# Attention on one core: where GpSimd's copy of the shared tail stands, and what it is written into

## What is computed

```python
hidden_states = jnp.concatenate([context, latents], axis=1)
q = (latents @ Wq).reshape(b, q_len, N_KV_HEADS, N_GROUPS, HEAD_DIM)
k = (hidden_states @ Wk).reshape(b, kv_len, N_KV_HEADS, HEAD_DIM)
v = (hidden_states @ Wv).reshape(b, kv_len, N_KV_HEADS, HEAD_DIM)
scores = jnp.einsum('bqhgd,bkhd->bhgqk', q, k) * scale
attn = jax.nn.softmax(scores.astype(jnp.float32), axis=-1).astype(q.dtype)
out = jnp.einsum('bhgqk,bkhd->bqhgd', attn, v)
```

## Time and profile before

| | |
|---|---|
| median of 3 runs | 3725.41 us (3724.01 to 3728.13) |
| the profiled execution | 3725.45 us, its span 3723.7 us |
| TensorE busy over the span | 3479.5 us (93%) |
| VectorE, ScalarE, GpSimd busy | 2323.2, 1415.3, 837.3 us |
| attention stage | about 1195 to 2005 us from the span's start |
| granted clock of TensorE | 0.973 in the mean; 1.00 in the middle of the attention |

### The profile page before, as it was taken

How to read it: one execution, slowest core, us unless ns; L and a number is a source line. 1 busy time by engine, 2 the same in 40 slices (tenths; PEclk the granted TensorE clock), 3 DMA queues, 4 the chain that set the end, 5 groups by cost and what they waited for, 6 DMA issues and landing times. The chain is left out here.

```text
span 3723.7 us, 52261 instructions
## 1 busy us (share of the span) xinstructions
PE 3479.5 (93%) x18370; PEld 3066.9 (82%) x18370; DVE 2323.2 (62%) x3935; ACT 1415.3 (38%) x2648; POOL 837.3 (22%) x1100
## 2 busy tenths in 40 slices
PE   6999999899999999999998999999799999699899
PEld 5888888799998888888887787787689999677676
DVE  5555575877665777777775333332578888566765
ACT  4333343444333777777775222221411111221321
POOL 0000000000002667666662100000011111233231
PEclk8999999899999999999999999999899999899999
DMA  3333333454444333333334545543334443698986
GB/s 124 100 105 97 99 98 90 115 134 115 121 121 124 103 108 90 105 104 108 105 86 145 144 118 154 154 119 93 110 116 150 143 154 137 254 287 277 302 285 199
DMA packets 525094, 520.73 MB, mean 140 GB/s; under 512 B 177668, under 2 KB 413188, under 8 KB 524884
## 3 DMA queue, kind: packets, MB, share of 16 engines
q1 hardware_dynamic: 489220, 391.06, 35.5%
q0 software_dynamic: 34608, 124.90, 10.1%
q10 hardware_dynamic: 1056, 2.10, 0.2%
HBM read 402.95 MB, written 115.02 MB: 139 GB/s over the span
## 5 line engine op out<-in xcount | busy, mean ns | idle before, releaser
L2083 PE MATMUL wo_acc<-wo_w,wo_l 128*128 128x512 f32 (+1 forms) x2496 | 573.7, 392 | 21.9 <-DVE wo_l L2033 21.8
L427 PE MATMUL kv_bank<-kv_wo,kv_so 128*128 128x512 f32 x2436 | 575.7, 396 | 15.8 <-DVE kv_wo L519 10.6
L2083 PEld LDWEIGHTS wo_acc<-wo_w,wo_l 128*128 128x128 f32 (+1 forms) x2496 | 460.2, 185 | 135.2 <-DVE wo_w L2057 24.7
L427 PEld LDWEIGHTS kv_bank<-kv_wo,kv_so 128*128 128x128 f32 x2436 | 458.7, 190 | 110.6 <-issue 16.7
L815 PE MATMUL pr_bank<-pr_xo,pr_wp 128*128 128x400 f32 x2688 | 500.6, 348 | 27.5 <-ACT pr_s L882 11.9
L815 PEld LDWEIGHTS pr_bank<-pr_xo,pr_wp 128*128 128x128 f32 x2688 | 495.4, 191 | 30.4 <-DVE pr_wp L899 22.6
L2312 PE MATMUL w_acc<-w_w,w_l 128*128 128x512 f32 (+1 forms) x1848 | 451.5, 404 | 60.9 <-DVE w_l L2287 60.0
L2312 PEld LDWEIGHTS w_acc<-w_w,w_l 128*128 128x128 f32 (+1 forms) x1848 | 344.8, 189 | 167.3 <-DVE w_l L2287 36.9
L26 PE MATMUL hid_acc<-x1t,hid_w 128*128 128x336 f32 x2688 | 442.6, 323 | 1.4 <-DVE c_raw L1827 0.9
L26 PEld LDWEIGHTS hid_acc<-x1t,hid_w 128*128 128x128 f32 x2688 | 426.4, 194 | 2.1 <-issue 1.1
L1311 PE MATMUL outs<-pt,v 128*128 128x384 f32 (+3 forms) x1536 | 347.3, 348 | 27.9 <-issue 14.0
(11 more groups left out here) (185 smaller groups left out, 4182.3 us busy)
## 6 DMA issues: line engine op xcount, KB each, us to landing
wo_l_raw<-o_scratch SPq DMA_DIRECT2D x192, 256.0 KB, 2.9
w_l_raw<-h_scratch SPq DMA_DIRECT2D x140, 256.0 KB, 4.6
pair_raw<-in_L_xattn_Wq_dram SPq DMA_DIRECT2D x64, 512.0 KB, 5.6
q_scratch<-pr_out SPq DMA_DIRECT2D x128, 200.0 KB, 2.4
o_scratch<-o_stage SPq DMA_DIRECT2D x64, 400.0 KB, 3.5
q_raw<-q_scratch SPq DMA_DIRECT2D x64, 384.0 KB, 3.2
stage<-in_ctx_dram SPq DMA_DIRECT2D x45, 512.0 KB, 3.9
h_scratch<-c_raw SPq DMA_DIRECT2D x28, 672.0 KB, 5.5
```

The costliest lines, as they stand in the source:

```text
L427: last = pe.matmul(bank[:, BANK[i], :], so[:, i, a, c, :], wo[:, i, e, c, :], start=(not opened and c == 0 and (a, e) == PAIRS[0]), stop=( ...
L2083: last = pe.matmul(acc[p][:rows, :], l[j % 2][:, a, k, :rows], w[:, c, m * per + k, :], start=(m == 0 and k == 0 and (a, c) == PAIRS[0]), ...
```

## The change

`pt` is replaced by three tiles: `pt_first` (384 columns, one buffer) for the first half of a group and `pt_second0` and `pt_second1` (416 columns) for the second half, of which even and odd groups use one each. The copy of the tail into the second half waits for the product of the group before last, which used the same buffer. In GpSimd's loop it stands behind the scaling of tile I where tile I - 4 is the second of the group. Matmuls, copies and their sizes stay as they are.

```diff
-        pt = sb("pt", [P, 2, NC, cols], F32R)
+        pt_first = sb("pt_first", [P, 2, NC, split], F32R)
+        pt_second = [sb(f"pt_second{i}", [P, 2, NC, cols - split], F32R) for i in range(2)]
...
         def pt_of(I, part):
-            _, _, t = place(I)
-            return pt_tail[:, part, :, :] if t is None else pt[:, part, :, t * P:(t + 1) * P]
+            _, G, t = place(I)
+            if t is None:
+                return pt_tail[:, part, :, :]
+            if t < TG // 2:
+                return pt_first[:, part, :, t * P:(t + 1) * P]
+            return pt_second[G % 2][:, part, :, (t - TG // 2) * P:(t - TG // 2 + 1) * P]
...
                 pool.wait_ge(pt_low, (G // groups) * NT + 1)
-                if G:
-                    pool.wait_ge(o_full, 2 * G)
-                pool.tensor_copy(pt[:, :, :, body:], pt_tail[:, :, :, g * left:(g + 1) * left]).then_inc(tail_in, 1)
+                if G >= 2:
+
+                    pool.wait_ge(o_full, 2 * (G - 1))
+                pool.tensor_copy(pt_second[G % 2][:, :, :, body - split:],
+                                 pt_tail[:, :, :, g * left:(g + 1) * left]).then_inc(tail_in, 1)
...
                 j = I - LAG - 1
-                if j >= 0 and place(j)[2] == 3:
+                if j >= 0 and place(j)[2] == 1:
                     bring_tail(place(j)[1])
...
-                    last = pe.matmul(outs[:, h, :hi - lo], v[b % 2][:n, a, k, g * P:(g + 1) * P], pt[:n, e, k, lo:hi],
+                    last = pe.matmul(outs[:, h, :hi - lo], v[b % 2][:n, a, k, g * P:(g + 1) * P],
+                                     (pt_first if h == 0 else pt_second[G % 2])[:n, e, k, :hi - lo],
```

## The result

| | before | changed |
|---|---|---|
| median | 3724.71 us (4 runs, 3720.31 to 3728.13) | 3678.57 us (4 runs, 3674.85 to 3683.52) |
| profiled execution, its span | 3723.7 us | 3673.1 us |
| attention: first start of an outs matmul | 1205.6 us | 1207.6 us |
| attention: start of the last copy out of `outs` | 2003.6 us | 1964.6 us |
| from the one to the other | 798.0 us | 757.0 us |

The ratio is 0.9878, with a 95% interval of 0.9861 to 0.9895: 46 us less, where 39.4 were forecast. 3678.57 lies 1.4 us under the range of 3680 to 3699. The direction and the stage are as predicted; the time of the whole lies outside the range.

What follows compares the result with a forecast made beforehand. TensorE was taken to bound the attention stage, with stalls of 40.4 us waiting for GpSimd's tail copy: 3725.4 - 40.4 = 3685.0, plus 1 us left for odd steps, forecast 3686 us (0.76). The range was 3680 to 3699 us.

Steps and rivals of the forecast that it cites:

- The waiting engine and what it waited for: Attention stage: TensorE bounds it, and its waits ahead of the outs matmuls are for GpSimd's copy of the tail.
- the 49 gaps: TensorE's idle pieces ahead of the outs matmuls, 32 labelled "issue" and 17 VectorE's pt; all claimed to await GpSimd's copy.
- The size of a stall, from starts: Second halves of groups: score start to transposes start on TensorE, less an undisturbed 1.47 us; 40.4 us in all.
- the idle column: Listed TensorE idle ahead of the outs matmuls, 27.9 us; as the true size, a rival giving 3697.5 us, within 0.12.
- What is late next, and GpSimd's queue: Group 2's second half: last tile's low part ready 0.89 us ahead; scaling behind the copy keeps 0.23 us, costed at nothing.
- The part that came back: Rival, 0.12 together with the idle-column form: GpSimd's queue behind the copy late in groups 1 and 2, 12 us, giving 3697.
- The margin of 0.23: Time in us left between GpSimd's scaling of tile 19, behind the moved copy, and TensorE's weight load for its transpose.
- 0.50 of 0.62 us: With group 1's stall gone TensorE comes 0.62 us earlier to tile 19's transpose; GpSimd was to follow by 0.50.
- the 0.75: Margin in us, before the change, between the end of tile 19's scaling on GpSimd and TensorE's weight load for its transpose.
- The second buffer is what lets it be early: GpSimd's copy into the second half: it now waits for the group before last, no longer the last group; about 12 us.
- Left 1 us for odd late steps: Added to the sum of 3685.0 because the 0.23 us margin is thin and a few steps may miss it; gives 3686.
- the stage's gain reaches the end whole: After attention the output projection starts behind a barrier and loads awaiting the last store, so all 40.4 us were to count.

Runs made afterwards that it cites:

- double_late: The changed kernel with the tail copy set back to its old place, new buffers kept; 3724.26 us, ratio to the kernel before 1.0002.
- copy_x4: The changed kernel with three more copies of the same size, into an unread tile, ahead of each tail copy; 3702.18 us, ratio to the kernel before 0.9949.
- single_early: The kernel before, one buffer pt kept, with only the tail copy moved two tiles earlier; 3683.17 us, ratio 0.9891.
- single_fifth: The kernel before, one buffer pt kept, with the tail copy one tile later; 3933.51 us in one run, ratio of some 1.058.

## Why the prediction was right, and where it was wrong

*The waiting engine and what it waited for:* right, for 47 of the 49 gaps; the two in the drain (0.9 us) wait for something else and stay. The changed place removed both kinds of the rest, `double_late` kept both, and its label names a tile that the waiting product doesn't read.

*The size of a stall, from starts:* right. 40.4 us were summed; the stage took 41.0 and 40.8 us less in the two pairs (its end moved by 39.0 and 41.2). The missing half a us and more is about what the one batch that was read leaves out: its idle before group 1's second half, 0.38 us, is one of the shortest of fifteen, whose mean is 0.43, and 0.05 x 15 is 0.7. By the idle column it would have been 27.9 and by that of the weight loads 50.5. The Trainium skill (Perfetto Trace Analysis, Identifying the Most-Contended Engine) calls matmul busy time a bad measure of how close TensorE is to its peak and takes the weight loads' busy share instead. This trace agrees on the first, since the matmuls' idle column is 13 us short; the idle column of the weight loads, which is not the page's measure, is some 10 us too long.

*What is late next, and GpSimd's queue:* right, with 0.88 and 0.39 us for the 0.89 and 0.23 forecast. The part that came back was nil; `copy_x4` shows that the mechanism exists and where it starts. The margin of 0.23 was mis-sized and measured 0.39: GpSimd followed TensorE in full and not by 0.50 of 0.62 us (v starts 2.67 us ahead of the weight load in both kernels), and the copy took 0.36 of the 0.75, not 0.40. By the Trainium skill (SBUF — State Buffer, Who interferes with whom) a VectorE instruction with two SBUF inputs contends with a GpSimd instruction that reads SBUF, and it is the order of issue that decides which of the two blocks the other; the prediction has VectorE's block GpSimd's only. The copies' lengths show no such case: 64 of them took 388 to 413 ns in the new place, 386 to 417 in the old.

*"The second buffer is what lets it be early":* wrong. I read what the wait is for and not when it ended. Three steps lie between the last third of one group's second half and the first third of the next one's, and the copy's turn comes within them even in the new place. `single_early` gives 0.9891, the changed kernel 0.9889.

*Left 1 us for odd late steps:* not needed.

*The range, and "the stage's gain reaches the end whole":* this is the step that failed. The sum took 40.4 us from one median and left everything outside the stage as it was, with no term for its scatter; the range was built as if only unknown costs inside the stage could move the result. It reaches down to 3680, 5 us under the sum of 3685.0. The runs show in its place that the time outside the stage is not fixed: behind the attention it was 1720.1 us in the execution that the forecast was read from, and 1708.5 to 1729.4 over all ten. Whole executions scatter too: the 12 of the kernel before in the second series go from 3713.28 to 3728.37, and the 8 of the changed kernel in both from 3674.85 to 3693.67; the three runs shown ahead of the prediction lay within 4.1 us. A median of four lies several us from that of the next four (3678.57 and 3682.33). The prediction itself names 7.5 us as what a measurement of this kernel can tell from no change, and gave the range nothing of it: 3685.0 - 7.5 = 3677.5 would have held the result.

As an estimate, of the 7.4 us between the forecast of 3686 and 3678.57, 1.0 is the allowance for odd steps, 0.7 the median of before (3724.71 beside this result, 3725.4 in the sum), and 0.6 the stage (41.0 and not 40.4). The other 5.1 lie outside the stage, in the scatter that no run explains. So it is luck on which side of 3680 a median of four fell: the next four, at 3682.33, are inside the range. The gain itself fits: the first interval, 0.9861 to 0.9895, holds the ratio that goes with 40.4 us (0.9892), and so does the second.

## What to carry to other kernels

A wait has a place in a queue as well as a condition: before buying a buffer for it, look at when the condition came true in the trace, and try the place alone. Price a stall by the distance between starts on the waiting engine against an undisturbed step, not by the idle column, and name its releaser from which instruction ended just before, not from the label. Give the range the scatter of executions on top of the unknown costs; three runs say little of it.

## What the runs showed of the hardware

Stalls of up to 0.9 us of idle, in three groups of four through 810 us, left TensorE's granted clock at 1.00. In `single_fifth`, with stalls of 2.0 to 2.8 us in all four groups, it fell to 0.50 for a time behind some of them, and a stage with 125 us more of idle was busy for 80 us more with the same work, at a mean clock of 0.91. The price of a late semaphore was then not linear in its lateness. No run lies between the two, so where the fall begins is open.
